# First read of a fused decoder layer: its normalisation on ScalarE out of PSUM, its weights loaded first

## The reference

```python
x = x + _L0_attn_ref(_layernorm(x, axis=-1), ...)
x = x + _L0_xattn_ref(_layernorm(x, axis=-1), ...)   # begins with rat_read(h, attn_read_w, g, b, 3)

def rat_read(res, W, gamma, beta, num_outputs):
    x = res.reshape(b, l, H, C)                      # H = 256, C = 4
    y = jnp.einsum('blhc,hoc->bloh', x, W)           # three outputs of 256 for each token
    mu = y.mean(-1, keepdims=True)
    var = y.var(-1, keepdims=True)
    yn = (y - mu) * jax.lax.rsqrt(var + EPS)
    yn = yn * gamma.reshape(num_outputs, H) + beta.reshape(num_outputs, H)
```

## Time and profile before

| what | us |
|---|---|
| median of three runs | 1933.74 |
| lowest and highest | 1928.92, 1940.87 |
| the profiled execution's own time | 1936.91 |
| its span | 1935.2 |
| busy in the span: TensorE, VectorE, ScalarE, GpSimd | 1617.2, 1364.9, 903.6, 576.7 |
| mean granted TensorE clock | 0.918 |

### The profile page before, as it was taken

One profiled execution on the slowest core, in us unless ns is written; L12 is line 12 of the kernel. 1 busy time (PEld: TensorE's weight loads), 2 busy tenths in 40 slices (PEclk: granted clock), 3 DMA queues, 4 the chain that ended last, 5 costly groups with the idle time before them and its releaser, 6 DMA issues. The chain is left out here.

```text
span 1935.2 us, 23526 instructions
## 1 busy us (share of the span) xinstructions
PE 1617.2 (84%) x6880; PEld 1062.2 (55%) x6880; DVE 1364.9 (71%) x2077; ACT 903.6 (47%) x1671; POOL 576.7 (30%) x460
## 2 busy tenths in 40 slices
PE   3679999999999899999999887558897567785599
PEld 2456666666666666666666654455564453343244
DVE  7558788777877777788788766664465775777851
ACT  2245445454454454544454442243467655667210
POOL 1045446345355355454455452103111000000000
PEclk9889999999999999999999999679899567887699
DMA  3111101101011111110101000406342000000111
GB/s 117 52 44 33 55 22 55 34 25 54 34 44 34 34 45 34 45 44 23 55 23 44 22 23 12 171 33 120 76 67 84 1 1 1 0 33 22 40 53 38
DMA packets 30982, 84.39 MB, mean 44 GB/s; under 512 B 6006, under 2 KB 7304, under 8 KB 30600
## 3 DMA queue, kind: packets, MB, share of 16 engines
q1 hardware_dynamic: 30856, 82.87, 14.6%
HBM read 70.27 MB, written 12.58 MB: 43 GB/s over the span
## 5 line engine op out<-in xcount | busy, mean ns | idle before, releaser
L492 DVE SCALAR_TENSOR_TENSOR acc<-pj,sc_o,acc 128x1024 f32<-128x1024 f32 x232 | 293.9, 1279 | 99.2 <-PE pj L623 92.4
L492 DVE SCALAR_TENSOR_TENSOR q_acc<-pj,sc_q,q_acc 128x1024 f32<-128x1024 f32 x224 | 286.7, 1280 | 40.3 <-PE pj L623 32.2
L602 POOL TENSOR_TENSOR prob<-prob,inv_total 128x512 f32<-128x512 f32 (+3 forms) x256 | 190.0, 746 | 400.1 <-DVE inv_total L537 400.1
L623 PE MATMUL pj<-ctx_hi,w_o 128*128 128x512 f32 x528 | 238.1, 451 | 28.7 <-DVE kv_acc L492 13.5
L623 PE MATMUL pj<-zT_hi,w_q 128*128 128x512 f32 x512 | 225.5, 441 | 2.4 <-DVE q_acc L492 2.0
L435 ACT ACTIVATE prob<-ps,low_max 128x512 f32<-128x512 f32 (+3 forms) x256 | 134.3, 527 | 163.4 <-DVE low_max L530 149.4
L676 PE MATMUL ps<-kT,qT 128*128 128x512 f32 (+3 forms) x512 | 187.2, 448 | 25.5 <-issue 14.0
L623 PE MATMUL pj<-ctx_lo,w_o 128*128 128x512 f32 x528 | 207.9, 394 | 0.0
L623 PE MATMUL pj<-zT_lo,w_q 128*128 128x512 f32 x512 | 203.6, 398 | 0.0
L700 PE MATMUL pv<-probT,v 128*128 128x512 f32 (+3 forms) x512 | 169.6, 433 | 0.0
L623 PEld LDWEIGHTS pj<-ctx_hi,w_o 128*128 128x128 f32 x528 | 99.1, 188 | 116.7 <-DVE acc L492 47.3
(11 more groups left out here) (309 smaller groups left out, 3116.5 us busy)
## 6 DMA issues: line engine op xcount, KB each, us to landing
raw_o<-in_w_o SPq DMA_DIRECT2D x33, 512.0 KB, 3.6
raw_q<-in_w_q SPq DMA_DIRECT2D x32, 512.0 KB, 3.6
x_ring<-qk_kept SPq DMA_DIRECT2D x64, 128.0 KB, 5.1
ln_x<-in_x SPq DMA_DIRECT2D x8, 512.0 KB, 6.5
raw_kv<-in_w_k SPq DMA_DIRECT2D x8, 512.0 KB, 3.5
raw_kv<-in_w_v SPq DMA_DIRECT2D x8, 512.0 KB, 3.9
x<-in_x SPq DMA_DIRECT2D x8, 512.0 KB, 6.4
x_kept<-x SPq DMA_DIRECT2D x8, 512.0 KB, 2.6
```

Of the source, the lines that this page charges most:

```text
L492: dve.scalar_tensor_tensor(out=dst, in0=pj[slot][:], scalar=scale, in1=dst, op0=ALU.mult, op1=ALU.add).then_inc(evac_v, 1)
L602: pool.tensor_tensor(prob[:, k % PROBS, 0:w], prob[:, k % PROBS, 0:w], inv_total[:, n:n + 1].to_broadcast([P, w]), ALU.mult).then_inc(norm ...
L623: ins = pe.matmul(pj[slot][:, b * S:(b + 1) * S], lhs, part[:, b * S:(b + 1) * S], start=n == 0, stop=n == 1)
```

## The change

Three edits, all in `residual_read` and its `Read` object. `Read` for the second read (in a later stage) keeps its old form.

1. The normalisation of the three read outputs moves from VectorE (three `tensor_scalar`, subtract and multiply) to ScalarE (three `activation` with `Identity`, scale = the reciprocal root, bias = the shift). VectorE computes the shift, minus mean times reciprocal root, in one instruction of 128x3. ScalarE's three stand after copy_h(i-1) and ahead of copy_y(i-2).
2. `rw1` leaves the nine loads and is issued alone between the angle loads and the tiles of x, with a semaphore of its own, `rw_in`. GpSimd makes the spread weights after that semaphore; its later copies of qkvT still wait for the remaining eight loads.
3. VectorE's wait for the remaining loads, with the decoder's two step instructions behind it, moves from round 1 to round 4.

```diff
@@ Read.finish and a new method
     def finish(self, dve, link, i):
         dve.wait_ge(self.sd_ready, i + 1)
         rsqrt_newton(dve, link, self.r[:, i], self.sd[:, i], self.mv[:, i, :, 1], self.t[:, i], LN_EPS)
+        if self.by_scalar:
+            dve.scalar_tensor_tensor(out=self.shift[:, i], in0=self.mv[:, i, :, 0], scalar=-1.0, in1=self.t[:, i],
+                                     op0=ALU.mult, op1=ALU.mult).then_inc(self.shift_done, 1)
+            return
...
+    def normalise(self, act, i):
+        act.wait_ge(self.shift_done, i + 1)
+        if i >= 2:
+            act.wait_ge(self.yt, self.nb * (i - 1))
+        for o in range(self.n_out):
+            act.activation(self.yn[i % 2][:, o * XH:(o + 1) * XH].rearrange("p (b k j) -> p b k j", b=2, j=32),
+                           self.y_view(i, o), ACT.Identity, bias=self.shift[:, i, o:o + 1],
+                           scale=self.t[:, i, o:o + 1]).then_inc(self.yn_done, 1)
@@ SyncE
             for dst, src in early:
                 sp.dma_start(dst, src).then_inc(angles_in, 16)
+            sp.dma_start(rw[:], rw_src).then_inc(rw_in, 16)
             for i in range(NT):
                 sp.dma_start(x1[:, i, :], x_t[i]).then_inc(loaded[i], 16)
@@ GpSimd
             pool.wait_ge(shaped, 2)
+            pool.wait_ge(rw_in, 16)
+            rd.weights(pool)
             pool.wait_ge(consts_in, 16 * len(loads))
-            rd.weights(pool)
@@ ScalarE
                 if i >= 2:
+                    rd.normalise(act, i - 2)
                     if i == 2:
                         act.wait_ge(consts_in, 16 * len(loads))
                     rd.copy_y(act, i - 2)
@@ VectorE
-                if i == 1:
+                if i == 4:
                     dve.wait_ge(consts_in, 16 * len(loads))
                     deq.make_steps(dve)
```

More of the change, by code:

```diff
@@ L799, with __init__ @@
 class Read:
-    def __init__(self, nc, ctx, name, h, rw, gam, bet, n_out, ident, eps, half_mask, inT, p_h, p_y, p_t, hT=None):
+    def __init__(self, nc, ctx, name, h, rw, gam, bet, n_out, ident, eps, half_mask, inT, p_h, p_y, p_t, hT=None, by_scalar=False):
         sb, psum, sem = scope(nc, ctx)
@@ L811, in __init__ @@
         self.sd, self.r, self.t = (sb(name + n, [P, NT, n_out]) for n in ("sd", "r", "t"))
+        self.by_scalar = by_scalar
+        if by_scalar:
+            self.shift, self.shift_done = sb(name + "shift", [P, NT, n_out]), sem(name + "shift")
         self.p_h, self.p_y, self.p_t = p_h, p_y, p_t
@@ L903, in residual_read @@
 def residual_read(nc, a, acc, ident, eps, x1, h, ident_r, mask, half_mask, ones, deq, loads, early, pos, inv, qkvT, swapT,
-                  cos_r, sin_r, rw, gam, bet, inT, x1_kept):
+                  cos_r, sin_r, rw, rw_src, gam, bet, inT, x1_kept):
     x_t = a["x"].rearrange("b (t p) d -> (b t) p d", p=P)
@@ L918, in residual_read @@
         p_t = [psum(f"r_pz{i}", [P, 512]) for i in range(2)]
-        rd = Read(nc, ctx, "r1", h, rw, gam, bet, 3, ident, eps, half_mask, inT, p_h, p_y, p_t)
+        rd = Read(nc, ctx, "r1", h, rw, gam, bet, 3, ident, eps, half_mask, inT, p_h, p_y, p_t, by_scalar=True)
         loaded = [sem(f"r_loaded{i}") for i in range(NT)]
@@ L922, in residual_read @@
             "chain", "turned", "added", "var", "sd", "done", "moved"))
-        made, shaped, angles_in, consts_in, ready, trig = (sem(f"a_{n}") for n in (
-            "made", "shaped", "in", "consts", "ready", "trig"))
+        made, shaped, angles_in, rw_in, consts_in, ready, trig = (sem(f"a_{n}") for n in (
+            "made", "shaped", "in", "rw", "consts", "ready", "trig"))
         block = ctx.enter_context(nc.Block())
@@ L2146, in program @@
             cos_r, sin_r = sbx("cos_r", [P, NT, P]), sbx("sin_r", [P, NT, P])
-            first = [(rw1[:], a["rw1"]), (g1[:], a["g1"]), (b1[:], a["b1"]), (rw2[:], a["rw2"]),
+            first = [(g1[:], a["g1"]), (b1[:], a["b1"]), (rw2[:], a["rw2"]),
                             (g2[:], a["g2"]), (b2[:], a["b2"]), (qkvT[:], a["qkvT"])] + deq.loads()
@@ L2156, in program @@
                               [(pos[:], a["pos"]), (inv[:], a["inv"])], pos, inv, qkvT, swapT, cos_r, sin_r,
-                              rw1, g1, b1, inT, x1_kept)
+                              rw1, a["rw1"], g1, b1, inT, x1_kept)
             ring = [sbx(f"x_ring{i}", [P, 2, GH, S], F32R) for i in range(2)]
```

## The result

| what | us |
|---|---|
| before, median of 19 runs | 1932.69 (1927.05 to 1941.04) |
| after, median of 19 runs | 1945.96 (1937.96 to 1951.71) |
| ratio, 95% interval | 1.0061 (1.0048 to 1.0074) |
| predicted | 1939.0 (1929.0 to 1950.0) |

The change makes the kernel slower by 0.6%: some 12 us by the ratio, 13.3 by the medians. That is inside the range and within 1% of before, but the loss is over twice the 5 us that the sum gave. The profiled execution of the changed kernel took 1951.71 us, the longest of the nineteen, and that of the kernel before 1936.91, some 4 us above its median; so rows of the two are compared here, and the whole times by their medians and the ratio.

The account below looks back on a forecast made before the run. No engine was full: a start stall and a chain from `stats` to `stats` through one PSUM tile, at TensorE's mixed clock, bounded the stage. -6.5 + 0.5 + 10.6 + 0.3 = +4.9 us gave 1939, range 1929 to 1950.

Parts of the forecast that it names:

- seven gaps: From `stats` of tile 0 to that of tile 7: 62.1 us before, forecast 72.7, so +10.6 us.
- the low clock's old share 0.46: How far the seven gaps lay from all-fast (2.4 GHz) to all-slow (1.2 GHz) before; the forecast kept it.
- eighth tile: Last tile, no `h` behind it: the change costs only the shift and a handover, +0.3 us.
- Part 1, the start: Before the first statistics: without VectorE's wait for the loads, the first `h` is ready 6.5 us earlier.
- The stall: VectorE's single 5.8 us wait at the stage's start for the last constant load, `d_lut`; forecast to go.
- Part 2, the weights beside the angles: GpSimd's spread weights run beside VectorE's 13 angle instructions and slow them: +0.5 us, bounds 0 and 1.7.
- Part 3, the normalisation on ScalarE: Three activations (1.48 us) queue behind the copies of `h`: each gap 1.15 us longer at high clock, 1.97 at low.
- VectorE is the bound: Rival: VectorE limits the rounds, each saves 1.2 us, about -15 us in all, 1919; chance 0.04.
- The start doesn't move: Rival: something else holds the first `h` or products until the loads are in; about +11 us, 1945; chance 0.07.
- High clock prevails: Rival: TensorE stays at 2.4 GHz in all rounds, gaps 62.8 us, total -5.0 us, 1929; chance 0.14.
- Low clock prevails: Rival: longer idle stretches keep TensorE at 1.2 GHz, gaps 84.4 us, total +16.6 us, 1950; chance 0.17.

Follow-up runs that it names:

- the loads' part alone: Kernel before plus only the loads' edits (early `rw1`, later wait for the other loads), normalisation left on VectorE: 1926.92 against 1932.69 us, ratio 0.9979.
- both sets of extra transposes: Changed kernel plus extra TensorE transposes, four ahead of the wait for `h` and eight behind `turn_h`: 1930.17 us, ratio to before 0.9984.
- The transposes behind `turn_h`: Changed kernel plus eight extra TensorE transposes in each of rounds 2 to 8, between `turn_h` and the turn of `r1yn`: 1932.18 us, ratio to before 0.9992.

## Why the prediction was right or wrong

The prediction's terms against the profile of the changed kernel:

| term | predicted | measured |
|---|---|---|
| start (first `h` earlier; weights beside the angles) | -6.5 + 0.5 = -6.0 | 18.67 - 24.83 = -6.2 |
| seven gaps, at the low clock's old share 0.46 | +10.6 | 7 x 8.85 + 0.46 x 7 x 3.07 - 62.1 = +9.7 |
| seven gaps, as they came | +10.6 | 78.50 - 62.10 = +16.4 |
| eighth tile | +0.3 | +0.2 |
| stage | +4.9 | +10.5 |

- **Part 1, the start: right.** The stall went, the late loads hid behind other work, and the part alone measured below before. The decoder's steps in round 4 cost nothing that the gaps show.
- **Part 2, the weights beside the angles: right in size,** 0.46 against 0.5, but not by the sum that was made: not some five instructions by 0.13 each, but eight by 0.03 to 0.09. The Trainium skill's exclusive lock ("SBUF — State Buffer", section "SBUF: two separate sides") made it 3.0 at worst. The trace doesn't agree with it here: one of the weights' eight instructions takes 0.35 us, and no angle instruction is held up by more than 0.09.
- **Part 3, the normalisation on ScalarE: right in mechanism and in its durations.** The three activations take 1.47 to 1.48 (predicted 1.48); the estimate of 1.57 from the Trainium skill, "ScalarE: Activation LUTs", section "What ACT_TABLE_LOAD costs", was 0.1 high. The gap is 8.85 us at the high level (seen only with the extra transposes) and 11.92 at the low, against 8.97 and 12.06. The order on ScalarE was the place of the price: moving the three ahead of the copies took 9 us off the gaps.
- **The step that failed: "With the low clock's share kept at 0.46".** The share is how far the seven gaps lie from the high level's price to the low level's. By the measured levels the share is (78.50 - 7 x 8.85) / (7 x 3.07) = 16.55 / 21.5 = 0.77. The forecast had listed the longer idle stretch as the ground of a rival (0.17) and then priced its own case as if that stretch had no effect. The additional 0.31 x 21.5 = 6.7 us, less about 0.9 because both levels came out a little lower than worked out, is the difference of 5.8 between the gaps predicted and measured. The transposes behind `turn_h` show what the clock costs: they add 56 instructions and give back 12.5 of the 16.4 us. What raised the share is shown less well. The move lengthened the stretch in front of the turn, and filling it raised the clock; but with the normalisation first the stretch was short and the clock no higher (0.62 against 0.66), so its length alone is not the cause.
- **Rivals.** "VectorE is the bound" is excluded; its idle time grew. "The start doesn't move" is excluded by the rows. "High clock prevails" did not happen by itself, but nearly its number came when TensorE was kept busy: -5.0 us predicted, -3.1 by the ratio with both sets of extra transposes. "Low clock prevails" was the nearer of the two: the gaps came out at +16.4, halfway between the forecast's +10.6 and that rival's +22.3. The time, +12 to +13, lies above the forecast's own 0 to +10, and inside the stated range, which reached up to that rival.
- **Idle time.** VectorE's wait before the statistics was to grow to some 35 us and grew to 41.7, the same surplus of low clock.
- **What the stage doesn't account for.** The stage gives +10.5, the ratio some +12, the medians +13.3. The rest is within what the unchanged parts of the program vary by from profile to profile; no experiment bears on it.

## What to carry to other kernels

Before work is moved to an idle engine, write out the chain through the buffer that it holds: here ScalarE, busy for 26 of 62 us, still made the gap from tile to tile 1.0 to 1.8 us longer at an equal clock, because its queue had two copies standing in front and the PSUM tile had no second buffer. With a second tile the same move paid. And don't carry a clock's share over from the profile before when the edit lengthens TensorE's idle stretches: price the rounds at both levels, and keep the range open to the lower one. Here the share rose from 0.46 to 0.77, which was the larger part of what the forecast missed.

## What the runs showed of the hardware beyond that

Idle time of TensorE could be dearer than work there: 56 extra transposes in stretches of 2.1 us raised the mean granted clock from 0.66 to 0.83 and made the kernel some 14 us faster by the medians. Twenty-four more, ahead of the wait for `h`, raised it to 0.93 and took another 2.6 us off the gaps, too little to see in the whole time. In the kernel with the loads' part alone the same twenty-four moved the clock only from 0.74 to 0.79, hardly more than two profiles of one kernel differ by (0.77 and 0.81), and the time not at all; the two kernels differ in more than this, and why the filling did less there is not shown. Nor is less idle time enough by itself: with the normalisation ahead of the copies TensorE was idle for some 20 us of the gaps instead of 30, and its clock was no higher, 0.62 against 0.66.
